# Adding an attention output bias on TensorE instead of GpSimd, with new instruction orders on all five engines

## The chip, the cores and the metric

One core of one Trainium2 chip runs the whole program. The metric is device time in microseconds (us) for one execution; three runs of the kernel before give the median. A span counted from the first to the last instruction is a little shorter than the device time. Engines are named as the profile names them: PE is TensorE's matmul side and PEld its weight loads, DVE is VectorE, ACT is ScalarE, POOL is GpSimd, SP is SyncE, which only issues transfers here. A trailing q (SPq) is an engine's queue.

## What is computed

Six blocks, each `x = layernorm(x + block(x))`, over x of 4 examples by 256 tokens by 256 features (8 tiles of 128 tokens):

```python
x = ln(x + attn0(x))     # linear attention, 16 heads: elu(q)+1, elu(k)+1; out @ o_w.T + o_b
x = ln(x + xattn0(x))    # 4 experts, chosen by token id: (silu(x Wg) * (x Wu)) Wd
x = ln(x + ffn0(x))      # 8 experts, all of them, weighted by "golden" weights
x = ln(x + attn1(x))     # 16 heads, causal softmax in groups of 32 tokens, half the heads rolled by 16
x = ln(x + xattn1(x))    # softmax over 256 memory rows of each example
x = ln(x + ffn1(x))      # 8 routed experts, top 2, and a shared one
```

Matrix products are done in three parts, with operands split into a high and a low part (hi·hi, hi·lo, lo·hi), to keep float32 accuracy. The change concerns `o_b`, the bias of the first attention's output product.

## The kernel before

The program is hand-written for the five engines, which meet only in semaphores. Tokens are handled in two halves of four tiles (h = 0, 1). The long part is a stream of 76 hidden chunks (chunk s = 0 to 75) in the three feed-forward blocks. For each chunk PE makes a gate product (step `g`) and an up product (step `u`, except in the first block, where the gate's input serves for both), six matmuls of 128x512 each; ACT takes silu (`s`); DVE multiplies (`m`, `hidden`); ACT writes the high part (`h`, `hidden_high`); POOL subtracts for the low part (`l`, `hidden_low`); PE multiplies by the down weights (`d`), and DVE adds the result to `x_tok` with an expert's weight (`a`). Weights come in raw by SP, are rounded to the high part by ACT and subtracted to the low part by POOL: steps `G` (gate and up weights of one pack), `D` (down weights) and `S` (weights of the second attention and of the memory rows); a number after the letter counts the packs, and on SP the same letter is the load itself. `X0` to `X3` do the same for the first block's experts.

Beside this stream run the steps with a dot, `letter half.number` (or `e example.number`): `b` the first attention, `n` and `r` layer norms and the golden routing, `e` norms and memory attention by example, `a h.i` the second attention and the last routing. `b h.9` is `a0_project`, the output product; `b1.8` transposes the attention output, which ACT and DVE split into `xp_hi` and `xp_lo`, for it. `p` are preparations at the start: DVE's `p5` converts the token ids into expert masks, and POOL's `p5` and `p6` are the two halves of the bias add. On DVE, `n h.0` (`a0_residual`, then `norm_stats`) adds the output product to `x_tok`; `r0.5` computes the golden weights, and `c` later constants.

What stands in what order on each engine is written out by hand in five lists: `SP_ORDER`, `PE_ORDER`, `ACT_ORDER`, `POOL_ORDER`, `DVE_ORDER`. Each engine walks its list; a step starts when the one ahead of it on the engine is done and its own semaphores are there, so a step that waits holds up all that stands behind it.

The output bias before: SP broadcasts `o_b` to all partitions (`bo1`, 128 KB). POOL adds it to the four tiles of each half of `x_tok` (L1241), and `a0_residual` waits for that (`x_biased`). The biases of keys and values already go another way: a weight operand `ones_r` with ones in three rows multiplies `b_kv`, whose row 0 holds the bias's high part and row 32 the low part, as one more matmul into the same accumulation (`ones_b`).

## Time and profile before

| | before |
|---|---|
| device time, median of three runs | 441.07 us |
| the three runs | 441.07, 441.37, 439.67 us |
| device time of the profiled execution | 441.07 us |
| its span, first to last instruction | 439.3 us |
| PE busy | 421.1 us |
| POOL, DVE, ACT busy | 271.5, 254.0, 246.9 us |

The profiled execution took 1.77 us more than its span, and its time is the median. Busy time says how full an engine was, not whether others waited for it; for PE the idle times in front of single instructions matter most, with what ended each. A matmul's modelled end lies behind the start of the next, so the idle time that a row shows is less than what the stream lost.

### The profile page before, as it was taken

To read this page: it belongs to the slowest core of one execution; us is meant where nothing else is said; L and a number is where in the kernel's file an instruction comes from. 1 tells how busy PE (TensorE), PEld (TensorE's weight loads), DVE (VectorE), ACT (ScalarE), POOL (GpSimd) and SP (SyncE) were. 2 spreads that over 40 slices of the span, in tenths; PEclk is the share of its full clock that TensorE was granted. 3 is DMA by queue.
4 is the path that set the end of the run, shared out by engine and by line. 5 is a ranking of instruction groups with operands and counts; after the bars stand their busy time and mean duration, and the time that the engine had idled before them with its cause. 6 is when DMAs were issued, how large, how long until landed. Compare 5 with 4: busy or idle time off the path is not lost.

```text
span 439.3 us, 9326 instructions
## 1 busy us (share of the span) xinstructions
PE 421.1 (96%) x3660; PEld 365.3 (83%) x3660; DVE 254.0 (58%) x641; ACT 246.9 (56%) x422; POOL 271.5 (62%) x237
## 2 busy tenths in 40 slices
...
DMA packets 15911, 35.32 MB, mean 80 GB/s; under 512 B 2139, under 2 KB 6235, under 8 KB 15868
## 3 DMA queue, kind: packets, MB, share of 16 engines
...
q8 instruction: 29, 0.48, 0.4%
q14 instruction: 14, 0.11, 0.1%
HBM read 33.15 MB, written 1.05 MB: 78 GB/s over the span
## 4 chain that ended last, share of the span: by engine, by line
PE 82%; DVE 10%; DMA 2%; issue 2%; ACT 2%; POOL 1%; SPq 1%; DVEq 0%; POOLq 0%; ACTq 0%
PE bank L455 13%; PE bank L456 13%; PE bank L458 13%; PE bank L717 8%; PE bank L719 7%; PE bank L718 7%; PE bank L736 2%; PE bank L793 1%; PE bank L781 1%; DVE hraw L1569 1%; DMA state<-o_tok 1%; PE bank L478 1%; DMA q_buf<-x_cols_dram 1%; PE bank L672 1%; PE bank L765 1%
## 5 line engine op out<-in xcount | busy, mean ns | idle before, releaser
L1257 POOL TENSOR_TENSOR h_lo<-hraw,h_hi 128x512 fp32r<-128x512 f32 x76 | 98.2, 1296 | 95.7 <-ACT h_hi L1048 95.7
L455 PE MATMUL bank<-xT_hi,pk_hi 128*128 128x512 f32 x256 | 103.3, 403 | 0.0
L456 PE MATMUL bank<-xT_hi,pk_lo 128*128 128x512 f32 x256 | 101.8, 398 | 0.8 <-issue 0.8
L1048 ACT ACTIVATE h_hi<-hraw 128x512 fp32r<-128x512 f32 x76 | 47.9, 630 | 76.6 <-DVE hraw L1569 72.6
L1263 POOL TENSOR_TENSOR pk_lo<-pk_raw,pk_hi 128x512 fp32r<-128x512 f32 (+1 forms) x44 | 74.6, 1696 | 10.3 <-ACT pk_hi L1066 10.3
L458 PE MATMUL bank<-xT_lo,pk_hi 128*128 128x512 f32 x256 | 80.9, 397 | 0.0
L717 PE MATMUL bank<-pk_hi,h_hi 128*128 128x256 f32 x272 | 77.9, 286 | 1.9 <-DVE x_tok L1583 1.3
L1569 DVE TENSOR_TENSOR hraw<-bank,sil 128x512 f32<-128x512 f32 x76 | 52.3, 689 | 45.9 <-ACT sil L1036 24.3
L719 PE MATMUL bank<-pk_hi,h_lo 128*128 128x256 f32 x272 | 76.8, 283 | 0.0
L718 PE MATMUL bank<-pk_lo,h_hi 128*128 128x256 f32 x272 | 76.8, 282 | 0.0
L458 PEld LDWEIGHTS bank<-xT_lo,pk_hi 128*128 128x128 f32 x256 | 48.5, 189 | 12.7 <-issue 1.0
L455 PEld LDWEIGHTS bank<-xT_hi,pk_hi 128*128 128x128 f32 x256 | 48.6, 190 | 10.3 <-issue 0.7
L1036 ACT ACTIVATE sil<-bank 128x512 f32<-128x512 f32 x76 | 44.7, 588 | 22.0 <-PE bank L458 21.9
L456 PEld LDWEIGHTS bank<-xT_hi,pk_lo 128*128 128x128 f32 x256 | 48.7, 190 | 10.1
L717 PEld LDWEIGHTS bank<-pk_hi,h_hi 128*128 128x128 f32 x272 | 51.8, 191 | 4.5 <-issue 2.3
L718 PEld LDWEIGHTS bank<-pk_lo,h_hi 128*128 128x128 f32 x272 | 51.9, 191 | 1.0
L719 PEld LDWEIGHTS bank<-pk_hi,h_lo 128*128 128x128 f32 x272 | 51.9, 191 | 0.0
L1268 POOL TENSOR_TENSOR pk_lo<-pk_raw,pk_hi 128x256 fp32r<-128x256 f32 (+1 forms) x44 | 41.5, 943 | 11.6 <-ACT pk_hi L1077 11.4
L1066 ACT ACTIVATE pk_hi<-pk_raw 128x640 fp32r<-128x640 f32 (+1 forms) x44 | 37.4, 849 | 18.2 <-PE bank L458 14.5
L1077 ACT ACTIVATE pk_hi<-pk_raw 128x256 fp32r<-128x256 f32 (+1 forms) x44 | 21.6, 492 | 28.1 <-PE bank L719 27.9
L1583 DVE SCALAR_TENSOR_TENSOR x_tok<-bank,gold,x_tok 128x256 f32<-128x256 f32 x64 | 27.4, 477 | 13.5 <-PE bank L719 13.5
L1549 DVE TENSOR_TENSOR sil<-bank,sil 128x512 f32<-128x512 f32 x22 | 15.2, 690 | 34.5 <-ACT sil L1036 17.7
...
## 6 DMA issues: line engine op xcount, KB each, us to landing
...
```

The lines of the kernel that those rows point to most:

```text
L455: pe.matmul(o, w(kc)[0], x(kc)[0], start=kc == 0, stop=False)
L456: pe.matmul(o, w(kc)[1], x(kc)[0], start=False, stop=False)
L458: m = pe.matmul(o, w(kc)[0], x(kc)[1], start=False, stop=kc == KC - 1)
L717: pe.matmul(o, hh, vh, start=closed and kc == 0, stop=False, skip_group_check=not closed)
L718: pe.matmul(o, hh, vl, start=False, stop=False, skip_group_check=not closed)
L719: m_ = pe.matmul(o, hl, vh, start=False, stop=closed and kc == chunks - 1, skip_group_check=not closed)
L1036: A(sil[:, s % 2, :], src[:, :], ACT.Silu).then_inc(sems["silu_done"], 1)
L1048: A(h_hi[:, row, at * 512:(at + 1) * 512], hraw[:, s % 2, :], ACT.Copy).then_inc(sems["hid_hi"], 1)
L1257: pool.tensor_tensor(h_lo[:, row, q], hraw[:, s % 2, :], h_hi[:, row, q].bitcast(F32), ALU.subtract).then_inc(sems["hid_lo"], 1)
L1263: pool.tensor_tensor(g_part(kind, i, pk_lo)[:, 0:w], raw_g(kind, i)[0][:, 0:w], g_part(kind, i, pk_hi)[:, 0:w].bitcast(F32), ALU.subtract) ...
L1268: pool.tensor_tensor(d_part(kind, i, pk_lo), raw_d(kind, i)[0], d_part(kind, i, pk_hi).bitcast(F32), ALU.subtract).then_inc(sems["d_lo"], 1)
L1569: TT(hraw[:, r, :], other[:, :], sil[:, r, :], ALU.mult).then_inc(sems["hid_mul"], 1)
```

## The change

The bias moves into the output product. `b_o`, a 128x256 slice of a buffer that is free then, gets the high part of `o_b` in row 0 (an additional ACT copy in `p0`) and the low part in row 32 (an additional DVE subtraction in `p0`), and `a0_project` gets one more matmul of 128x256 for each of the eight tiles. The row of biases grows from 512 to 768 columns. SP's broadcast of `o_b`, POOL's two adds and their semaphores go; `a0_residual` waits for `x_tok` itself to be loaded.

All five lists are written anew, most of their lines differing. The diff, with two lines of each kind of the lists:

```diff
 SP_ORDER = """
-G0 D0 G1 D1 S0 G2 D2 G3 D3 G4 D4 G5 S1 D5 ...
+S0 G0 D0 G1 D1 S1 G2 D2 G3 D3 G4 D4 G5 D5 ...
...
 POOL_ORDER = """
-p1 p5 p3 p4 p6 X0 X1 X2 X3 n0.0 G0 D0 l0 l1 n1.0 ...
+p1 p3 p4 n0.0 X0 X1 X2 X3 l0 l1 n1.0 l2 l3 l4 l5 S0 l6 l7 l8 G0 D0 ...
...
-        bo1 = sb("bo1", [P, D])
-        brow = sb("brow", [P, 2 * D])
+        brow = sb("brow", [P, 3 * D])
+        b_o = pr_lo[:, 0, :]
...
-            sp.dma_start(bo1[:, :], bias_o.partition_broadcast(P)).then_inc(sems["in_bo"], 16)
...
-                        m = pe.matmul(o, al, wh, start=False, stop=kc == KC - 1)
+                        pe.matmul(o, al, wh, start=False, stop=False)
+                    m = pe.matmul(o, ones_r, b_o, start=False, stop=True)
...
-                    A(b_kv[0:BZ, :], brow[0:BZ, :], ACT.Copy).then_inc(sems["bz_hi"], 1)
+                    A(b_kv[0:BZ, :], brow[0:BZ, 0:2 * D], ACT.Copy).then_inc(sems["bz_hi"], 1)
+                    A(b_o[0:BZ, :], brow[0:BZ, 2 * D:3 * D], ACT.Copy).then_inc(sems["bz_hi"], 1)
...
-                if i >= 5:
-                    q = slice(HT * (i - 5), HT * (i - 4))
-                    pool.wait_ge(sems["in_x"], 16)
-                    pool.wait_ge(sems["in_bo"], 16)
-                    pool.tensor_tensor(x_tok[:, q, :], x_tok[:, q, :], bo1[:, :].unsqueeze(1).to_broadcast([P, HT, D]),
-                                       ALU.add).then_inc(sems["x_biased"], 1)
...
-                    dve.wait_ge(sems["bz_hi"], 1)
-                    TT(b_kv[GS:BZ, :], brow[GS:BZ, :], b_kv[GS:BZ, :].bitcast(F32), ALU.subtract
+                    dve.wait_ge(sems["bz_hi"], 2)
+                    TT(b_kv[GS:BZ, :], brow[GS:BZ, 0:2 * D], b_kv[GS:BZ, :].bitcast(F32), ALU.subtract)
+                    TT(b_o[GS:BZ, :], brow[GS:BZ, 2 * D:3 * D], b_o[GS:BZ, :].bitcast(F32), ALU.subtract
                        ).then_inc(sems["bz_lo"], 1)
...
-                dve.wait_ge(sems["x_biased"], h + 1)
+                if h == 0:
+                    dve.wait_ge(sems["in_x"], 16)
```

Three places of the lists matter below. First DVE, where the first attention ends and the first block begins. Before, `n0.2` (`xT_lo`), then `p5` (the eight small instructions), then `b1.8` (`xp_lo`) and `m0`, `m1` (`hraw`):

```order
L1411 TENSOR_TENSOR xT_lo<-bank,xT_hi 128x2x256 x2
L1444 RECIPROCAL temp<-temp 128x1
L1445 CAST ids_f<-ids_i 128x8
L1448 TENSOR_SCALAR route<-ids_f 128x8
L1450 TENSOR_SCALAR s<-ids_f 128x8
L1451 SCALAR_TENSOR_TENSOR route<-ids_f,s 128x8
L1450 TENSOR_SCALAR s<-ids_f 128x8
L1451 SCALAR_TENSOR_TENSOR route<-ids_f,s 128x8
L1452 TENSOR_SCALAR route<-ids_f 128x8
L1539 TENSOR_TENSOR xp_lo<-bank,xp_hi 128x512 x2
L1569 TENSOR_TENSOR hraw<-bank,sil 128x512 x2
```

and now:

```order
L1407 TENSOR_TENSOR xT_lo<-bank,xT_hi 128x2x256 x2
L1537 TENSOR_TENSOR xp_lo<-bank,xp_hi 128x512 x2
L1440 RECIPROCAL temp<-temp 128x1
L1441 CAST ids_f<-ids_i 128x8
L1444 TENSOR_SCALAR route<-ids_f 128x8
L1446 TENSOR_SCALAR s<-ids_f 128x8
L1447 SCALAR_TENSOR_TENSOR route<-ids_f,s 128x8
L1446 TENSOR_SCALAR s<-ids_f 128x8
L1447 SCALAR_TENSOR_TENSOR route<-ids_f,s 128x8
L1448 TENSOR_SCALAR route<-ids_f 128x8
L1567 TENSOR_TENSOR hraw<-bank,sil 128x512 x2
```

`p5` moved behind `xp_lo`, and still stands ahead of `hraw`.

Second ACT at the same place of the program. Before, from the second half's attention queries on (`b1.3`, `G0`, `n0.1`, `n0.2`, `D0`, `b1.8`, `s0`, `h0`, `s1`, `h1`):

```order
L1023 ACTIVATE q_buf<-bank,bcol 128x512
L1066 ACTIVATE pk_hi<-pk_raw 128x1024 [waits raw_g0]
L961 ACTIVATE x_tok<-x_tok,shift,rstd 128x256 [waits ln_rstd]
L961 ACTIVATE x_tok<-x_tok,shift,rstd 128x256 x3
L937 ACTIVATE xT_hi<-bank 128x2x256 [waits xt_ps] x2
L1077 ACTIVATE pk_hi<-pk_raw 128x512 [waits raw_d0]
L1027 ACTIVATE xp_hi<-bank 128x512 [waits a0_aT_ps] x2
L1036 ACT_TABLE_LOAD
L1036 ACTIVATE sil<-bank 128x512 [waits gate_ready]
L1048 ACTIVATE h_hi<-hraw 128x512 [waits hid_mul]
L1036 ACTIVATE sil<-bank 128x512 [waits gate_ready]
L1048 ACTIVATE h_hi<-hraw 128x512 [waits hid_mul]
```

and now:

```order
L938 ACTIVATE xT_hi<-bank 128x2x256 [waits xt_ps] x2
L1029 ACTIVATE xp_hi<-bank 128x512 [waits a0_aT_ps] x2
L1038 ACT_TABLE_LOAD
L1038 ACTIVATE sil<-bank 128x512 [waits gate_ready]
L1068 ACTIVATE pk_hi<-pk_raw 128x1024 [waits raw_g0]
L1079 ACTIVATE pk_hi<-pk_raw 128x512 [waits raw_d0]
L1050 ACTIVATE h_hi<-hraw 128x512 [waits hid_mul]
L1038 ACTIVATE sil<-bank 128x512 [waits gate_ready]
L1050 ACTIVATE h_hi<-hraw 128x512 [waits hid_mul]
L1085 ACTIVATE wa_hi<-kv_buf 128x2x768 [waits a0_o_ps,raw_s]
L1038 ACTIVATE sil<-bank 128x512 [waits hid_mul,gate_ready]
```

`G0` and `D0` moved in between the first silu and the first `h_hi`, and `S0` (`wa_hi<-kv_buf`), which stood behind `s8`, behind the second `h_hi`.

Third PE in the second attention's first half. Before, the end of the queries' product (`a0.3`) and the start of the keys' (`a0.4`):

```order
L458 MATMUL bank<-xT_lo,wa_hi 128x512 x2
L455 MATMUL bank<-xT_hi,wa_hi 128x512 [waits a1_q]
L456 MATMUL bank<-xT_hi,wa_lo 128x512
L455 MATMUL bank<-xT_hi,wa_hi 128x512
L456 MATMUL bank<-xT_hi,wa_lo 128x512
```

and now:

```order
L458 MATMUL bank<-xT_lo,wa_hi 128x512 x2
L455 MATMUL bank<-xT_hi,pk_hi 128x512 [waits silu_done,g_lo]
L456 MATMUL bank<-xT_hi,pk_lo 128x512
L455 MATMUL bank<-xT_hi,pk_hi 128x512
L456 MATMUL bank<-xT_hi,pk_lo 128x512
L458 MATMUL bank<-xT_lo,pk_hi 128x512 x2
L455 MATMUL bank<-xT_hi,wa_hi 128x512 [waits a1_q]
```

The gate product `g35` moved from ahead of `a0.3` to between the two. In the same way `g36` moved to between `a0.6` and `a0.7`, and `e0.12`, `e1.12` from behind `g34` to ahead of it; in the second half of the tokens `a1.3` and `a1.4`, and `a1.6` and `a1.7`, still follow each other directly.

## Rows read from the trace of the kernel before

**Rows 1.** The page: busy share of the engines, and the chain that ended last.
```profile
PE 421.1 (96%) x3660; PEld 365.3 (83%) x3660; DVE 254.0 (58%) x641; ACT 246.9 (56%) x422; POOL 271.5 (62%) x237
PE 82%; DVE 10%; DMA 2%; issue 2%; ACT 2%; POOL 1%; SPq 1%; DVEq 0%; POOLq 0%; ACTq 0%
```
**Rows 2.** The timeline, output product `b0.9`: start, duration, engine, line, instruction.
```profile
28.88 0.28 PE L592 MATMUL bank<-wa_hi,h_hi 128*128 128x256 f32 x1
28.99 0.28 PE L593 MATMUL bank<-wa_lo,h_hi 128*128 128x256 f32 x1
```
**Rows 3.** The timeline, from `n0.2` to `b1.9`; idle time in brackets.
```profile
41.01 1.28 DVE L1411 TENSOR_TENSOR xT_lo<-bank,xT_hi 128x512 fp32r<-128x512 f32 x2
...
42.20 0.15 DVE L1444 RECIPROCAL temp<-temp 128x1 f32<-128x1 f32 x1
...
44.25 1.29 DVE L1539 TENSOR_TENSOR xp_lo<-bank,xp_hi 128x512 fp32r<-128x512 f32 x2
...
45.59 0.39 PE L592 MATMUL bank<-wa_hi,xp_hi 128*128 128x256 f32 x1 [1.21 <-DVE xp_lo L1539]
```
**Rows 4.** The timeline: `X2`, `X3` low parts, `n0.0`, `G0`, `l0`, `S0`.
```profile
28.83 2.54 POOL L1232 TENSOR_TENSOR xp_lo<-pk_raw,xp_hi 128x512 fp32r<-128x512 f32 x2
...
34.85 1.02 POOL L1217 TENSOR_TENSOR rstd<-var_e,mhalf 128x4 f32<-128x4 f32 x1 [3.49 <-DVE var_e L1380]
...
35.91 1.06 ACT L1066 ACTIVATE pk_hi<-pk_raw 128x1024 fp32r<-128x1024 f32 x1
...
46.88 1.29 POOL L1257 TENSOR_TENSOR h_lo<-hraw,h_hi 128x512 fp32r<-128x512 f32 x1 [3.80 <-ACT h_hi L1048]
...
66.39 1.48 ACT L1083 ACTIVATE wa_hi<-kv_buf 128x1536 fp32r<-128x1536 f32 x1
```
**Rows 5.** The view of L375, SP's loads of gate packs: issue to landing.
```profile
DMA to landing us min/median/max: 3.5/3.7/5.5
```
**Rows 6.** The timeline: a bias add on POOL, and DVE beside the other.
```profile
16.04 1.00 DVE L1524 SCALAR_TENSOR_TENSOR q_buf<-kx,q_buf 128x512 f32<-128x512 f32 x1 [1.56 <-ACT q_buf L1023]
...
21.54 2.40 POOL L1241 TENSOR_TENSOR x_tok<-x_tok,bo 128x1024 f32<-128x1024 f32 x1
```
**Rows 7.** The timeline: the norm `r1.0` on DVE, then `d9` on PE.
```profile
110.02 1.34 DVE L1380 TENSOR_SCALAR var_e<-mv 128x4 f32<-128x4 f32 x1
110.04 1.30 POOL L1268 TENSOR_TENSOR pk_lo<-pk_raw,pk_hi 128x512 fp32r<-128x512 f32 x1
...
112.28 0.36 PE L717 MATMUL bank<-pk_hi,h_hi 128*128 128x256 f32 x1 [0.50 <-DVE x_tok L1583]
```
**Rows 8.** The timeline: `D7` and `l31` on POOL, `d14` and `d15` on PE.
```profile
161.09 0.35 PE L717 MATMUL bank<-pk_hi,h_hi 128*128 128x256 f32 x1 [0.76 <-DVE x_tok L1583]
...
162.16 1.30 POOL L1268 TENSOR_TENSOR pk_lo<-pk_raw,pk_hi 128x512 fp32r<-128x512 f32 x1
163.42 1.28 POOL L1257 TENSOR_TENSOR h_lo<-hraw,h_hi 128x512 fp32r<-128x512 f32 x1
...
164.80 0.35 PE L717 MATMUL bank<-pk_hi,h_hi 128*128 128x256 f32 x1 [0.61 <-issue]
```
**Rows 9.** The timeline, PE: start of `a0.3`, of `a0.4` and of `a0.7`.
```profile
178.85 0.47 PE L455 MATMUL bank<-xT_hi,wa_hi 128*128 128x512 f32 x1 [0.19 <-issue]
...
182.72 0.50 PE L455 MATMUL bank<-xT_hi,wa_hi 128*128 128x512 f32 x1 [0.84 <-DVE q_buf L1647]
...
196.29 1.56 PE L781 MATMUL bank<-kx,q_buf 64*32 64x128 f32 x64 [0.58 <-DVE kv_buf L1664]
```
**Rows 10.** The timeline at `a0.11`; busy time of PE, PEld, DVE, ACT, POOL, clock, DMA.
```profile
224.00 0.58 SPq L375 DMA_DIRECT2D pk_raw<-pk_f_dram  x1
...
226.98 0.27 PE L793 MATMUL bank<-kv_buf,pT 32*32 32x17 f32 x10 [1.05 <-issue]
...
227.00:231.00 4.00, 4.00 (x20) 3.15 (x20) 1.97 (x4) 1.49 (x3) 1.28 (x1) 0.57 0.04 13
```
**Rows 11.** The timeline, PE: start of `e3.2`.
```profile
340.88 0.84 PE L478 MATMUL bank<-con,x_tok 128*128 128x128 f32 x4 [0.39 <-ACT x_tok L951]
```

More of the change, by code:

```diff
@@ L113 @@
 SP_ORDER = """
[L114 to L115 removed]
+S0 G0 D0 G1 D1 S1 G2 D2 G3 D3 G4 D4 G5 D5 G6 D6 G7 D7 G8 D8 G9 D9 G10 D10 G11 S2 D11 G12 S3 D12 G13 D13 G14 D14 R0 G15
+R1 D15 G16 G17 G18 S4 G19 G20 G21 G22 G23 G24 G25 G26 R2 G27 R3 G28 G29 G30 G31 G32 G33 G34 G35 G36 G37 G38 G39 G40
 G41 G42 G43 O0
```

86 lines of the change are left out of this document (42 added, 44 removed).

## Prediction, made before the changed kernel ran

> **What bounds the kernel now.** I read the busy line and the chain first [rows 1]: PE is busy for 421.1 of 439.3 us, and 82% of the chain that ended last is PE, 10% DVE. So the time is PE's own work, plus the places where PE waits, plus a start and an end that the change leaves alone. An engine at 56 to 62% counts only where PE waits for it. A matmul that is added to PE costs its whole length; one that is moved costs nothing by itself. After that I read, instruction by instruction, the rows of PE that show idle time, and for each what stands ahead of the releaser on its own engine.
>
> How much an idle row is worth: in the output product the starts of 128x256 matmuls lie 0.12 us apart (28.88 to 28.99, and on average 0.12), while one is modelled with 0.28 us [rows 2]. Idle time counts from that modelled end, so a wait has cost the stream 0.16 us more than its row shows. I use this for all rows of PE below.
>
> **The added matmuls.** Eight of 128x256 at 0.12 us: +0.96 us. Nothing hides them. The four in `b0.9` also push everything behind it, since queries, state and norm follow from it in a chain; the four in `b1.9` come after.
>
> **The small pieces in p0.** An additional ACT copy and an additional DVE subtraction on 33 rows and 1 row. No row has them. Between nothing and one 128x512 DVE instruction (0.64, half of the pair in [rows 3]) they delay the key and value biases; I take 0, since a row-wide instruction of half that width is about 0.4 and the first matmul that needs them comes later than that after the existing subtraction. Upper bound: +0.3.
>
> **What goes from POOL.** Two adds of 2.40 us each [rows 6]. PE waits for neither, and nothing of weight is queued behind them. Beside the first one DVE's `q_buf` instruction took 1.00 us [rows 6], and the second of its kind there waits for ACT anyway. Value: 0; it could be up to 0.3 if some instruction beside them was on the chain. The broadcast load is worth nothing either.
>
> The Trainium skill ("SBUF — State Buffer", section "Who interferes with whom") says that GpSimd and VectorE share one port pair, held exclusively for a whole instruction. By that rule the long `q_buf` instruction is one that waited for the bias add, and its gain is real but off the path, as the sum has it.
>
> **p5 behind b1.8 on DVE.** Before, the id conversion ran from 42.20 to 44.25, between `xT_lo` and `xp_lo`, and PE stood idle for 1.21 us in front of `b1.9` [rows 3], so it lost 1.37. Now `xp_lo` follows `xT_lo`: it ends at 42.29 + 1.29 = 43.6, plus 0.48 of bias matmuls 44.1. PE is due at 45.59 - 1.37 + 0.48 = 44.7. The wait is gone: **-1.37**. Next late is PE itself. The 2 us of `p5` now lie ahead of the first `hraw`; that one then ends near 46.8, before PE's `g2`, which needs it at about 48.1.
>
> **G0 and D0 ahead of h0 on ACT.** Here the new order has a price. POOL made the low parts of `X2`, `X3` before 31.4 [rows 4], and SP issued the loads of `G0` and `D0` then. Now `n0.0` stands ahead of all four: it begins at 34.85 + 0.48 and takes 1.3 us with its second instruction, then four times 1.27 us (half of 2.54) end at 41.7. The load of `G0` is issued then and lands 3.7 us later, 3.5 at best and 5.5 at worst [rows 5]: at 45.4. ACT then rounds `G0` (1.06) and `D0` (about 0.6) and only then takes `h0`, at 47.2 or a little later, instead of 46.2. `h0`, `s1`, the product on DVE and `h1` follow in turn (four steps of about 0.65), then `l1` with 1.29 [rows 4]: done near 51.3. PE is due at `d0` at 44.7 + 28 times 0.12 + 2.8 for `g2`, `g3` = 50.9. That is a wait of 0.35 (0.1 of it already at `g3`). Behind `h1` now stands `S0`, 1.48 us [rows 4], and the second norm's `n1.1` comes later by that and by the later `h` steps: `n1.2` on PE loses about 0.6. Together **+0.95**.
>
> **The norm r1.0 and d9.** Before, `a8` stood behind `r1.0` and PE lost 0.50 + 0.16 at `d9` [rows 7]. Now `a8` stands ahead of it, and PE reaches `d9` later; but `m20` stands behind the norm and `u22` needs it. The norm's small DVE instructions are slow only while POOL works: `var_e` took 1.34, from 110.02 until POOL's instruction of 110.04 ended at 111.34 [rows 7]. With POOL busy for one of the two such instructions I get a wait of 0.3 at `u22`, with both 1.3, with none 0. **-0.66 + 0.3**.
>
> **D7, l31, d14, d15.** `r1.5` and `a13` stay as they were, and so does the wait in front of `d14` [rows 8]. At `d15` POOL did `D7` (1.30) ahead of `l31`, which could have started about 0.4 earlier; `D7` now is done before it. **-0.4**.
>
> **The second attention.** The start of `a0.3` at 178.85 hangs on DVE's constants and low parts, not on PE; now `g35` (six matmuls, 1.4) is still owed at that point, and the transposes of `e1.12` moved ahead wait as well. Between `a0.3` and `a0.4` PE lost 0.84 + 0.16 = 1.0 [rows 9], which `g35` now fills: +1.4 - 1.0 = **+0.4**. Between `a0.6` and `a0.7` it lost 0.58 + 0.16 [rows 9], and `g36` covers all of it: **-0.74**. The second half's pair of such waits has nothing put in and stays. At `e3.2` PE lost 0.39 + 0.16 [rows 11]; two down products now stand between the earlier steps and it: **-0.55**.
>
> **The sum.** +0.96 - 1.37 + 0.95 - 0.36 - 0.4 + 0.4 - 0.74 - 0.55 = **-1.11 us**. The profiled run took 441.07, of which 439.3 is span, and is itself the median: 441.07 - 1.11 = 440.0. With the open prices at their ends (0.3 of `p0`, -0.3 on POOL, `u22` 0 to 1.3, the load 3.5 to 5.5) the forecast's own range is 438.7 to 441.6.
>
> **Rivals.** (A) *The instruction stall does not come back.* In `a0.11` PE stood for 1.05 us ("issue") while a load issued at 224.00 was in flight, and in the four us from 227 on the granted clock was 0.57, between the two levels of 1.2 and 2.4 GHz [rows 10]. That cost 1.2 + 4 x 0.43 = 2.9 us. PE's order there is unchanged and `D13`, `G14`, `G15` keep their places, which speaks for a repetition; but a shift of 1 us between load and matmuls may dissolve it, and one of the three runs was 1.4 us below the median. Time: 437.1.
>
> (B) *The gain at b1.9 does not come.* `b1.9` could wait for ACT's `xp_hi` or for the first norm instead. The rows show ACT ahead of DVE there, which speaks against. Then only the matmuls and the loads' order are left: 440.0 + 1.37 = 441.4.
>
> (C) *ACT's queue stands behind weights that are not there, the slower side.* If `G0` lands after 5.5 us instead of 3.7, `h0`, `l1` and `d0` come 1.8 later, all of it on PE; `D0`, issued behind it, can land up to 0.4 later still, and the same pattern comes again where `D2`, `G3` stand ahead of `h18`, for about 0.8 at `g21`. 440.0 + 3.0 = 443.0. It decides from a landing after about 46 us. The load is alone with that of `S0`, which speaks against.
>
> Where a page's rule would give another time: the skill's rule of the exclusive port would make both small instructions of `r1.0` wait if POOL has `l18` and `l19` back to back. That is the upper end (1.3 at `u22`), inside the forecast; the trace agrees with it at 110.02.
>
> **Chances.** Forecast 0.45, A 0.25, B 0.15, C 0.15. 0.5% (2.2 us) is about what a measurement of this kernel can tell from no change: 438.9 and 443.3 are the bounds. Faster: A and a little of the forecast, 0.30. Slower: the upper half of C and what I overlook in 2000 moved rows, 0.12. Same: 0.58. The range for 8 in 10 takes in A at its centre and most of C: 437.0 to 442.9; the forecast's own range stands above.
>
> **What would show each step.** Eight matmuls with `pr_lo` in the output products, 0.12 apart. No idle time in front of the second product's first matmul. `G0`'s rounding on ACT starting near 45.5, `h0` at 47.2, a short wait of PE before the first `L718` matmul, and one at the transposes of `n1.2`. No idle before `d9`, a short one at `u22`. `a0.3` waiting and `a0.4` not; `a0.7` not; in the second half both still idle with 0.84 and 0.58. The stall in `a0.11` and the clock after it as before. The forecast is wrong if a new idle time of over 1 us stands anywhere in PE's row, above all between 46 and 60 us, or if the stall and the low clock are gone.

## The result, and the profile after

| | before | after |
|---|---|---|
| median | 441.22 us (4 runs, 439.67 to 441.51) | 448.05 us (4 runs, 446.67 to 448.8) |
| profiled execution | 441.07 | 447.0 |
| its span | 439.3 | 445.2 |

The ratio is 1.0152, with a 95% interval of 1.0122 to 1.0182: the change costs 6.8 us. Forecast were 440.0, and 437.0 to 442.9. The record lists 23 executions of the changed kernel in all; without the two slow ones (452.24 and 452.65) their median is 447.51, so the four of the table lie about 0.5 high, and with them what is counted from 448.05 below. The page of the profile after begins with these busy times; the last line is from the chain that ended last [rows 1]:

```profile
PE 425.5 (96%) x3668; PEld 368.0 (83%) x3668; DVE 256.1 (58%) x642; ACT 247.3 (56%) x423; POOL 265.5 (60%) x235
...
PE 70%; DVE 10%; ACT 6%; POOL 5%; DMA 4%; issue 3%; SPq 1%; ACTq 0%; DVEq 0%; POOLq 0%
```

POOL lost its two adds and is 6.0 us less busy. PE's share of the chain fell from 82% to 70%: other engines now stand in it. To find where, I compared PE's start times at the points at which both kernels have done the same set of steps. The time is the start of the next step, with its wait. How much later the changed kernel is there:

| both have done everything up to | before, us | later by |
|---|---|---|
| `b0.1` | 13.1 | +1.14 |
| `b0.9` | 31.7 | +1.59 |
| `g1`, ahead of `b1.9` | 45.6 | +0.20 |
| `g5` | 58.0 | +1.89 |
| `u20` | 112.3 | +1.22 |
| `u31`, then `d14` | 161.1, 164.8 | +2.27, +2.87 |
| `e1.12`, then `u34` | 175.6, 177.1 | +3.66, +5.07 |
| `a0.3` | 182.7 | +3.72 |
| `a0.6` | 196.3 | +2.88 |
| `a0.26` | 232.9 | +2.12 |
| `d25`, then `a1.10` | 307.2, 317.5 | +2.39, +3.12 |
| `g60`, then `e3.7` | 358.5, 360.9 | +4.16, +4.87 |
| `a1.24`, and at the end | 376.1 | +5.89, +5.95 |

No single place did it. Some gains came as forecast, and about ten losses of 0.3 to 1.6 us came too, most of them not in the sum. The timeline's rows (start, duration, engine, line, instruction; idle time in brackets) show each kind once.

**At the start** the new one-row subtraction in `p0`, and the bias matmul of `b0.1` behind it:

```profile
9.42 1.29 POOL L1229 TENSOR_TENSOR wa_lo<-pk_raw,wa_hi 128x512 fp32r<-128x512 f32 x1 [7.95 <-ACT wa_hi L972]
9.46 1.53 DVE L1473 TENSOR_TENSOR pr_lo<-brow,pr_lo 1x256 fp32r<-1x256 f32 x1
...
11.13 0.47 PE L494 MATMUL bank<-pr_hi,pr_lo 128*128 128x512 f32 x1 [0.41 <-DVE pr_lo L1473]
```

256 numbers took VectorE 1.53 us. POOL's instruction had started 0.04 earlier, and the small one ended 0.28 after it.

**At the first block** ACT waits for the load of `G0`, then for that of `D0`, and only then takes `h0` (L1050) [rows 4, 5]; PE waits at `g3` and `d0`:

```profile
46.93 1.06 ACT L1068 ACTIVATE pk_hi<-pk_raw 128x1024 fp32r<-128x1024 f32 x1 [0.84 <-DMA pk_raw<-pk_f_dram]
...
48.55 0.63 ACT L1079 ACTIVATE pk_hi<-pk_raw 128x512 fp32r<-128x512 f32 x1 [0.56 <-DMA pk_raw<-pk_f_dram]
...
49.09 0.61 ACT L1050 ACTIVATE h_hi<-hraw 128x512 fp32r<-128x512 f32 x1
...
50.97 0.50 PE L455 MATMUL bank<-xT_hi,pk_hi 128*128 128x512 f32 x1 [0.26 <-DVE hraw L1567]
...
53.00 0.39 PE L718 MATMUL bank<-pk_hi,h_hi 128*128 128x256 f32 x1 [0.38 <-POOL h_lo L1253]
```

**In the routing** `r1.5` on VectorE two tiny instructions took 1.32 and 1.19 us instead of 0.19 and 0.17, each beside a POOL instruction (`D7`, `l29`). Before, only one of `r1.5` was long, `none_in` with 1.26 us. Now `d14` starts behind 1.82 us of idle time instead of 0.76 [rows 8]. Below it the windows from 161 us on, in the columns of [rows 10] (PE, PEld, DVE, ACT, POOL, granted clock, DMA share, GB/s):

```profile
156.74 1.29 POOL L1264 TENSOR_TENSOR pk_lo<-pk_raw,pk_hi 128x512 fp32r<-128x512 f32 x1 [2.98 <-ACT pk_hi L1079]
156.75 1.32 DVE L1610 TENSOR_TENSOR fb<-fb,pick 128x32 f32<-128x32 f32 x1
...
158.21 1.29 POOL L1253 TENSOR_TENSOR h_lo<-hraw,h_hi 128x512 fp32r<-128x512 f32 x1 [0.18 <-ACT h_hi L1050]
158.33 1.19 DVE L1612 TENSOR_SCALAR s<-s 128x4 f32<-128x4 f32 x1
...
163.36 0.36 PE L718 MATMUL bank<-pk_hi,h_hi 128*128 128x256 f32 x1 [1.82 <-DVE x_tok L1581]
```

```profile
161.00:163.00 2.00, 0.54 (x3) 0.10 (x1) 1.86 (x7) 0.54 (x2) 0.00 (x0) 1.00 0.01 4
163.00:165.00 2.00, 1.64 (x12) 1.67 (x13) 1.59 (x4) 0.95 (x3) 1.29 (x1) 0.89 0.00 0
165.00:167.00 2.00, 2.00 (x11) 2.00 (x11) 0.87 (x2) 0.25 (x1) 1.67 (x2) 0.50 0.00 0
```

Behind PE's pause the granted clock fell to 0.50, the lower of its two levels (1.2 instead of 2.4 GHz). This fall belongs to that execution: nine profiles of the experiments below have the same order here and the same 1.99 to 2.00 us lost at `d14`, and a granted clock of 1.00 behind it. In them `d15` still loses 0.41 to 0.43 and `e1.12` 1.24 to 1.26; in the profile of the changed kernel the stretch at the low clock hid all of the first and part of the second (0.51).

**At the second attention** `S1`'s low part on POOL lies on VectorE's constants `c`: the instruction L1455 took 1.64 us, before 0.69. `a0.3` (L455) stands behind 1.34 us of idle time [rows 9]:

```profile
176.39 2.37 POOL L1274 TENSOR_TENSOR xp_lo<-kv_buf,xp_hi 128x1024 fp32r<-128x1024 f32 x1
...
177.67 1.64 DVE L1455 TENSOR_SCALAR cap<-cap 128x1024 f32<-128x1024 f32 x1
...
182.18 0.47 PE L455 MATMUL bank<-xT_hi,wa_hi 128*128 128x512 f32 x1 [1.34 <-issue]
```

**Late in the second half** order alone costs. On POOL, `e3.1`'s two tiny instructions (L1219, L1220) stand behind the low parts of `D25` and `G26` though VectorE had their input (L1389) at 340.05, and PE waits at `e3.2` [rows 11]. On ACT the silu `s62` stands behind `G33`, which waits 3.76 us until PE's `u62` frees its room; the product `g64` waits for it:

```profile
339.89 0.16 DVE L1389 TENSOR_SCALAR var_e<-mv 128x2 f32<-128x2 f32 x1
339.91 1.28 POOL L1259 TENSOR_TENSOR pk_lo<-pk_raw,pk_hi 128x512 fp32r<-128x512 f32 x1
341.15 0.71 POOL L1219 TENSOR_TENSOR rstd<-var_e,mhalf 128x2 f32<-128x2 f32 x1
...
342.91 0.84 PE L478 MATMUL bank<-con,x_tok 128*128 128x128 f32 x4 [0.79 <-ACT x_tok L952]
...
377.97 0.74 ACT L1068 ACTIVATE pk_hi<-pk_raw 128x640 fp32r<-128x640 f32 x1 [3.76 <-PE bank L458]
...
380.33 0.60 ACT L1038 ACTIVATE sil<-bank 128x512 f32<-128x512 f32 x1
...
381.96 0.48 PE L455 MATMUL bank<-xT_hi,pk_hi 128*128 128x512 f32 x1 [0.86 <-DVE hraw L1567]
```

### The profile page after: what moved, and what is told of

It reads as the page before. It is cut to its first block, busy times and chain, and to the rows that moved or that the text cites. A ratio compares the mean times of both kernels' runs of the same rounds, so it can differ in the third digit from the quotient of the medians.

```text
span 445.2 us, 9339 instructions
## 1 busy us (share of the span) xinstructions
PE 425.5 (96%) x3668; PEld 368.0 (83%) x3668; DVE 256.1 (58%) x642; ACT 247.3 (56%) x423; POOL 265.5 (60%) x235
## 3 DMA queue, kind: packets, MB, share of 16 engines
HBM read 33.05 MB, written 1.05 MB: 77 GB/s over the span
## 4 chain that ended last, share of the span: by engine, by line
PE 70%; DVE 10%; ACT 6%; POOL 5%; DMA 4%; issue 3%; SPq 1%; ACTq 0%; DVEq 0%; POOLq 0%
PE bank L455 12%; PE bank L456 11%; PE bank L458 11%; PE bank L718 7%; PE bank L720 7%; PE bank L719 7%; DMA pk_raw<-w_attn_dram 1%; PE bank L782 1%; DVE stats L1383 1%; DVE hraw L1567 1%; DMA state<-o_tok 1%; PE bank L737 1%; PE bank L794 1%; DMA pk_raw<-pk_f_dram 1%; ACT L1038 1%
## 5 line engine op out<-in xcount | busy, mean ns | idle before, releaser
L455 PE MATMUL bank<-xT_hi,pk_hi 128*128 128x512 f32 x256 | 103.0, 402 | 1.4 <-DVE hraw L1567 1.1
L1050 ACT ACTIVATE h_hi<-hraw 128x512 fp32r<-128x512 f32 x76 | 47.8, 629 | 77.4 <-DVE hraw L1567 72.1
L718 PE MATMUL bank<-pk_hi,h_hi 128*128 128x256 f32 x272 | 78.8, 290 | 2.2 <-DVE x_tok L1581 1.8
L455 PEld LDWEIGHTS bank<-xT_hi,pk_hi 128*128 128x128 f32 x256 | 48.5, 189 | 12.8 <-issue 1.7
L719 PEld LDWEIGHTS bank<-pk_lo,h_hi 128*128 128x128 f32 x272 | 52.8, 194 | 0.9
```

Of the source, the lines that this page charges most:

```text
L455: pe.matmul(o, w(kc)[0], x(kc)[0], start=kc == 0, stop=False)
L718: pe.matmul(o, hh, vh, start=closed and kc == 0, stop=False, skip_group_check=not closed)
L719: pe.matmul(o, hh, vl, start=False, stop=False, skip_group_check=not closed)
L1050: A(h_hi[:, row, at * 512:(at + 1) * 512], hraw[:, s % 2, :], ACT.Copy).then_inc(sems["hid_hi"], 1)
```

## Experiments

Ratios are to the kernel before, run on the same chip in the same rounds, with 95% intervals. The changed kernel itself didn't run in these rounds, so a gain against it is a difference of two such ratios. Single executions of one kernel spread over 2 to 7 us, so of effects under 1.5 us the traces tell more than the medians. "Lost" is what PE's start-to-start spacing exceeds its usual one by.

### The two halves of the change, and its late half

`e1`: all five new lists, bias by POOL.

```diff
-p1 p3 p4 n0.0 X0 X1 X2 X3 ...
+p1 p5 p3 p4 p6 n0.0 X0 X1 X2 X3 ...
```

> All five new orders, with the bias still added by GpSimd (its two adds stand where they stood before, ahead of the first low parts) and no bias matmuls. Theory 1 (most of the loss comes from what the new orders put beside and ahead of each other): about 4.8 us over the kernel before, 446.0, since of the 6.8 us lost the bias part explains 0.96 for the matmuls and about 1.1 for its two small pieces at the start. Theory 2 (the bias part delays the start, and the orders lose only because they then meet the engines in other phases): within 1 us of the kernel before. In the trace theory 1 wants the waits before d14, a0.3 and g64 to be there, theory 2 wants them gone.

448.4 us, ratio 1.0154 [1.0113, 1.0196]: the orders alone cost what the whole change costs, and more than the 4.8 us of theory 1. The waits before `d14`, `a0.3` and `g64` are there.

`e2`: the bias as matmuls, lists of before (POOL without `p5`, `p6`).

> The bias as matmuls, with the orders of before (less the two GpSimd adds). Theory 1: the matmuls cost 8 x 0.12 = 0.96, and the small subtraction of the low part of o_b (one row of 256), which took 1.53 us beside a GpSimd instruction in the changed kernel, costs 0.57 more, and the first two products another 0.5: +2.0 over the kernel before, 443.2. The prediction's own view (the small pieces are free): +0.96, 442.2. Rival: the bias part is the whole loss, 447 or more.

441.55 us, ratio 1.0006 [0.9978, 1.0033]. PE is 1.10 us later than before at the end of `b0.1`, and 2.05 after `b1.9`; at `u20`, where before it waited, 0.66 is absorbed, and 0.91 is left at the end. So the bias part is a small cost, and not the loss. The +2.0 us of theory 1 lie outside the interval (-1.0 to +1.5), the +0.96 inside it.

`e4`: the changed kernel, from about 240 us with the lists of before.

```diff
 PE    ... u46 g47 
-u47 d22 e0.7 e1.7 d23 a0.22 g48 u48 g49 u49 e2.12 e3.12 g50 u50 ...
+e0.7 u47 d22 e1.7 d23 a0.22 g48 u48 g49 u49 g50 u50 e2.12 e3.12 ...
```

> The changed kernel up to about 240 us, and from there on the five lists of before (from u47 on PE, G16 on ACT and POOL, a22's neighbour e0.7 on VectorE). Theory 1 (each place loses by its own local order): the 3.8 us that PE's stream lost between 232 us and the end go, -3.8 against the changed kernel, 444.2. Theory 2 (the late waits are the echo of the 2 us by which PE was already late there, or of weights that come later): at most 1 us is won, 447 or more.

441.81 us, ratio 1.0002 [0.9979, 1.0026]. Theory 1 wins: the late half costs 4.0 us between the two traces, as it asked, and 6.2 in the medians (5.7 against 447.51). By the medians the first 240 us of the change net nothing, within about 1 us; by its trace `e4` is 1.9 us behind the kernel before there, and 2.0 at the end.

### The late half in pieces

`e9`: one step of ACT.

```diff
-h61 G31 a1.22 D31 G32 D32 G33 D33 s62 a1.24 h62
+h61 G31 a1.22 D31 G32 s62 D32 G33 D33 a1.24 h62
```

> The changed kernel with one step moved on ScalarE: s62 back ahead of D32. Theory (G33 on ScalarE waits for weight room that PE's u62 gives back, and s62, whose gate product is done at 376.5, stands behind it until 380.3): s62 near 376.5, no wait in front of g64, -1.0, 447.0. Rival: g64 waits for the low parts of G33 next, which GpSimd makes at 378.8 to 380.1, or m62 waits for VectorE's a1.23: under 0.3 is won.

446.03 us, ratio 1.0133 [1.0064, 1.0201]; the median alone doesn't decide it. The trace speaks against the rival: in it `s62` starts at 376.07, as soon as its product is there, the wait at `g64` is gone, and PE gains 1.1 us at that place and keeps it:

```profile
376.07 0.60 ACT L1038 ACTIVATE sil<-bank 128x512 f32<-128x512 f32 x1 [1.32 <-PE bank L458]
```

`e10`: the lists of before for the memory attention's stretch alone.

```diff
 ACT   ... G23 D23 h53 s54 G24
-D24 G25 h54 s55 h55 s56 e2.1 h56 s57 D25 G26 e2.2 e3.1 e3.2 D26 G27 D27 G28 D28 h57 ...
+h54 s55 D24 G25 D25 G26 h55 s56 h56 D26 G27 e2.1 e3.1 e2.2 e3.2 s57 h57 s58 ...
```

> The changed kernel with the lists of before for the stretch of the second half's memory attention alone (PE from a1.11 to u60, ScalarE and GpSimd from D24 on, VectorE from m55 to o60). Theory (the losses at e3.2, e3.5 and e3.7 are of this stretch's own order, the weight steps D26 to D28 put ahead of h57 among them): 2.2 us, the sum of what the trace lost there, 445.8; the wait at g64 stays. Rival: the losses come in from ahead of the stretch (a1.10, g54), and under 0.7 is won.

445.02 us, ratio 1.0097 [1.0055, 1.0139]. The losses at `e3.2` (0.95), `e3.5` (0.53) and `e3.7` (0.32) are gone, and PE gains 2.5 us between `d29` and `u60`. The wait at `g64` stays.

`e16`: the lists of before from 232 to 326 us alone.

> The changed kernel with the lists of before for the stretch from 232 to 326 us alone (PE from e0.7 to a1.25/u54, ScalarE from G16 or S3 on, GpSimd from G16, VectorE from e0.7; SP's S4 behind G22). Theory (besides the 0.5 lost at g54 and 0.5 at the memory transposes, the changed order puts a1.10's burst of small matmuls ahead of d28 and stalls there by 2.6 us in some executions, as in two of eight profiles of such orders, which the medians see and the profile of the changed kernel does not): 1 us in the trace and 2 to 3 in the median, 445 to 446. Rival (the three parts of the late lists only win together): under 1, 447.5.

446.18 us, ratio 1.0095 [1.0066, 1.0125]: 2.5 us by the ratios. Its trace gains 1.1 up to `d28`; then instruction stalls of 0.90 and 1.19 at `a1.25` and `a1.11` took it back in that execution. The theory's stall at `a1.10` is not the order's: it stands in two of nine profiles with the new order there (2.58 in `e1`, 2.84 in `e6`), and in one of ten with the old (1.98 in `e3`). Against 447.51 the median gains 1.3 us, about what the trace shows; against 448.05 some 0.5 more, for which no trace speaks. The three pieces give 0.19, 0.55 and 0.57% by the ratios, together 1.31%; `e4` gave 1.50%. With intervals of 0.3 to 0.7% each, this neither shows nor excludes that they simply add up.

### The early places

`e17`: everything about the first weights as before. `e8` had been a first try, which moved `G0`, `D0` and `S0` on ACT and `n0.0` on POOL, but not `X0` to `X3` on ACT, nor the load of `S0`, which the change put ahead of that of `G0`.

```diff
 SP, e17 only
-S0 G0 D0 G1 D1 S1
+G0 D0 G1 D1 S0 S1
 ACT, e17 only
-b1.0 b0.8 b1.1 p4 X0 X1 X2 X3
+p4 b1.0 X0 X1 b0.8 X2 X3 b1.1
 POOL (e17: also G0 D0 ahead of l0, S0 behind l8)
-n0.0 X0 X1 X2 X3
+X0 X1 X2 X3 n0.0
 ACT, both
-n0.1 n0.2 b1.8 s0 G0 D0 h0 s1 h1 S0 ...
+G0 n0.1 n0.2 D0 b1.8 s0 h0 s1 h1 ... s8 S0
```

> The changed kernel with the first weights where they stood: G0 ahead of n0.1 and D0 ahead of b1.8 on ScalarE, S0 behind s8 there, and n0.0 behind X3 on GpSimd. Theory (G0 and D0 ahead of h0 made h0 49.1 instead of 46.2, and cost 0.42 at g3 and 0.54 at d0): both waits go, PE is 1.0 us earlier at 55 us, 447.0 if all of it is kept. Rival: n0.0 behind X3, or S0 behind s8, makes another wait (the first norm, n1.2) and the gain is under 0.3; or the later wait at d14 takes it back.

457.81 us, ratio 1.0364 [1.0325, 1.0403], 10 us worse. SP issued `G0` only at 39.06, behind `S0`, which waits for the attention's state, and ACT stood in front of `G0` with the norm behind it:

```profile
38.69 0.33 SPq L387 DMA_DIRECT2D kv_buf<-w_attn_dram  x1
39.06 0.43 SPq L375 DMA_DIRECT2D pk_raw<-pk_f_dram  x1
...
44.47 1.06 ACT L1068 ACTIVATE pk_hi<-pk_raw 128x1024 fp32r<-128x1024 f32 x1 [7.06 <-DMA pk_raw<-pk_f_dram]
```

That cost PE 5.55 us, in front of `n0.2`. The other large loss, 3.97 at `g10`, has a second cause: on POOL `S0` had been left ahead of `l6` while ACT's `S0` went behind `s8`, so POOL stood still and `l6` with it:

```profile
75.88 3.45 POOL L1270 TENSOR_TENSOR wa_lo<-kv_buf,wa_hi 128x1536 fp32r<-128x1536 f32 x1 [6.06 <-ACT wa_hi L1085]
```

> The changed kernel with everything about the first weights as before: on ScalarE the stretch from p4 to s8 (X0 to X3 early, G0 ahead of n0.1, D0 ahead of b1.8, S0 behind s8), on GpSimd n0.0 behind X3, G0 and D0 ahead of l0, S0 behind l8, and on SP the load of S0 behind D1. In e8 SP issued G0's load only at 39.06, behind that of S0 at 38.69, which waits for the attention state, and ScalarE stood 7.06 us in front of G0. Theory: the loads are issued near 31.5 again, no wait at n0.2, g3, d0 and g10, -1.0 in the trace at 55 us, 447.1. Rival: S0's low part on GpSimd, or the second load S1 on SP, is now late and G2's load with it: a wait at g10 or later of over 1 us.

445.23 us, ratio 1.0080 [1.0055, 1.0104]. So the theory holds and the rival, a wait of over 1 us at `g10` or later, didn't come. The load is issued at 32.56, and the waits at `g3` and `d0` are gone: 1.3 us in the trace between `b1.8` and `g5`. The ratio gained 0.72%, 3.2 us (2.3 against 447.51). Against `e9`, which is the changed kernel up to 370 us, 0.9 more show up at 225 us, but that is a smaller stall in `a0.25` (1.09 lost instead of 1.97), and not the order; what the medians have beyond the 1.3 stays unexplained.

`e7`: `D7` and `G8` back behind `h29`.

```diff
 ACT
-h28 s29 D7 G8 h29 s30 h30 s31 h31 D8
+h28 s29 h29 s30 h30 s31 D7 h31 G8 D8
 POOL
-D7 l29 l30 l31
+l29 l30 D7 l31
```

> The changed kernel with D7 and G8 on ScalarE back where they stood (D7 behind s31, G8 behind h31) and D7 on GpSimd back behind l30. Theory (GpSimd's D7 and l29, now free to run at 156.7 to 159.5, fall on two tiny instructions of the routing r1.5 on VectorE, which make r1.5 a microsecond longer and d14 late): r1.5 takes 6.9 us again, d14 loses about 0.8 instead of 1.98, the granted clock of 0.5 behind it is gone: -1.1 to -1.7 where it stands, 446.5 if the rest of the way keeps it. Rival 1 (l29 falls into r1.5 wherever D7 is, since it comes when h29 comes): r1.5 stays at 7.9 us and nothing is won, 448. Rival 2: d14 is won, and the later wait at a0.3, which hangs on VectorE, takes it back: 448 with a0.3 losing 2.5 instead of 1.5.

445.73 us, ratio 1.0114 [1.0051, 1.0177], which alone can't be told from the changed kernel. In the trace `r1.5` is a microsecond shorter: of its small instructions only one meets POOL, as before the change, and `d14` loses 0.94 instead of 1.98. At `d15` 0.76 comes back, as before the change. About 0.7 is left at `e0.12`, and rival 2 didn't come (`a0.3` loses 1.52 as before). The low clock, the second hope of the expectation, was no loss of the order: it was the profiled execution's own, about 1 us.

```profile
154.84 1.29 POOL L1253 TENSOR_TENSOR h_lo<-hraw,h_hi 128x512 fp32r<-128x512 f32 x1 [0.88 <-ACT h_hi L1050]
...
154.89 1.27 DVE L1608 TENSOR_SCALAR none_in<-s 128x4 f32<-128x4 f32 x1
...
162.51 0.35 PE L718 MATMUL bank<-pk_hi,h_hi 128*128 128x256 f32 x1 [0.77 <-DVE x_tok L1581]
```

`e6`: `S1` back behind `s34` on ACT and `l33` on POOL. `e11`: also `S2` behind `s35` and `l34`.

```diff
 ACT (e11)
-s18 S1 D2 ... h33 s34 S2 a0.4 D10 G11 h34 s35 h35
+s18 D2 ... h33 s34 S1 a0.4 D10 G11 h34 s35 S2 h35
```

> The changed kernel with S1, the first weights for the memory attention, back behind s34 on ScalarE and behind l33 on GpSimd. Theory (S1's low part on GpSimd at 176.4 to 178.8 lies on VectorE's constants c and makes them 5.8 us long instead of 4.7): c takes 4.7 us, a0.3 loses 0.4 instead of 1.51, -1.1, 446.9. Rival: the wait at a0.3 is for the low parts of the normed input, which come after c on VectorE and hang on GpSimd's other work too; then c shrinks by under 0.4 and the time stays, 448.

452.36 us, ratio 1.0251 [1.0192, 1.0310]. The theory was right on VectorE (`cap` 0.69 us, `bk_four` 0.23, and `a0.3` loses nothing) and wrong on the sum: `S2`'s load is issued when `S1`'s low part is done, and on ACT `S2` stood ahead of `a0.4`, on which `a0.5` waits:

```profile
176.87 0.69 DVE L1454 TENSOR_SCALAR cap<-cap 128x1024 f32<-128x1024 f32 x1
177.60 0.23 DVE L1455 TENSOR_SCALAR bk_four<-con,bcol 128x4 f32<-128x4 f32 x1
...
192.55 1.06 ACT L1091 ACTIVATE xp_hi<-kv_buf 128x1024 fp32r<-128x1024 f32 x1 [6.25 <-DMA kv_buf<-pk_x_dram]
...
196.43 0.55 PE L765 MATMUL bank<-wa_hi,xT_hi 128*128 128x256 f32 x1 [5.15 <-ACT kx L1115]
```

> The changed kernel with both memory weights moved: S1 behind s34 (ScalarE) and l33 (GpSimd) as in e6_S1_back, and S2 behind s35 and l34, so that ScalarE's a0.4 no longer stands behind S2. Theory (e6's 5.31 us in front of a0.5 came from S2, which stood ahead of a0.4 on ScalarE and waited 6.25 us for a load that is issued only when S1's low part is done; the constants c are 4.7 us or less without S1 beside them, as e6 showed with 3.7): no wait at a0.5, a0.3 without its 1.51, 1.3 us won at 200 us, 446.8. Rival (a0.5 waits for the moved keys for another reason, say the transfers between partitions): the wait at a0.5 stays above 2.

447.32 us, ratio 1.0137 [1.0091, 1.0183]. Neither `a0.3` nor `a0.5` waits, and 1.5 us are won up to `a0.7`; then `d17` loses 1.10, since `l35` now comes behind `S2`'s low part on POOL and ends at 200.5. The rival didn't come. Each of these steps had been placed for the others.

### The small subtraction, and PE's stalls

`e5`: `e2`, with `o_b`'s low subtraction as a step of its own behind `b0.7` on VectorE.

```diff
-                    dve.wait_ge(sems["bz_hi"], 2)
-                    TT(b_kv[GS:BZ, :], ..., ALU.subtract)
-                    TT(b_o[GS:BZ, :], ..., ALU.subtract).then_inc(sems["bz_lo"], 1)
+                    dve.wait_ge(sems["bz_hi"], 1)
+                    TT(b_kv[GS:BZ, :], ..., ALU.subtract).then_inc(sems["bz_lo"], 1)
+                elif i == 6:
+                    dve.wait_ge(sems["bz_hi"], 2)
+                    TT(b_o[GS:BZ, :], ..., ALU.subtract).then_inc(sems["bz_lo"], 1)
```

> The bias as matmuls with the orders of before, as in e2_matmul_alone, and in addition the small subtraction of o_b's low part taken out of the start: it is a step of its own on VectorE behind b0.7, with its own count, and only the output product waits for it. Theory (in e2 this one-row subtraction took 1.52 us, since it starts beside a GpSimd subtraction of 1.28, and PE's stream stood 1.10 us behind the kernel before at the end of b0.1): the one-row subtraction takes about 0.4 in its new place, PE is within 0.2 of the kernel before at the end of b0.1, so 0.9 earlier than in e2; of this some 0.7 may be lost again at later waits, as e2 lost 2.0 by 49 us and had 0.9 of it at the end: 440.8 to 441.5, e2 less 0 to 0.9. Rival (the additional ScalarE copy, which pushes the next weights' high part by 0.4, is what is late): under 0.3 is won at b0.1.

440.20 us, ratio 0.9976 [0.9949, 1.0003]: the theory holds at `b0.1`, the rival doesn't, and the median is a little below the range that was expected. The same instruction in the two kernels, `e2` first:

```profile
9.43 1.52 DVE L1472 TENSOR_TENSOR pr_lo<-brow,pr_lo 1x256 fp32r<-1x256 f32 x1
```

```profile
23.99 0.41 DVE L1476 TENSOR_TENSOR pr_lo<-brow,pr_lo 1x256 fp32r<-1x256 f32 x1
```

At the end of `b0.1` PE is 1.17 us ahead of `e2` and level with the kernel before.

`e13`: the kernel before, with six loads cut to 64 columns; it leaves the rest of these weights out and serves for the stalls alone.

```diff
-                    sp.dma_start(to, pk_f0[i % E0, :, 0:G_F0]).then_inc(landed, 16)
+                    n = 64 if i >= 13 else G_F0
+                    sp.dma_start(to[:, 0:n], pk_f0[i % E0, :, 0:n]).then_inc(landed, 16)
```

> The kernel before, in which the loads of the last three packs of the first routed block (G13 to G15, D13 to D15) carry 64 columns each instead of 1024 and 512; the packs keep old weights in the rest, so this kernel leaves that part of the weights out and its time is read only for PE's stalls. Theory (transfers of weights beside PE's many small matmuls delay its instructions): the two stalls of 1.00 and 1.23 us lost at u40 and in a0.11 go, and the low clock behind them, 3 us less, 438. Rival (the burst of small matmuls runs PE out of instructions by itself, since another run of the changed orders stalled 2.4 us at a1.10 with a DMA share of 0.00 to 0.04): the stalls stay, within 0.3 us each, 441.

441.73 us, ratio 1.0015 [0.9983, 1.0048]: the rival holds. The stalls stand where they stood, with 1.07 and 1.21 us lost, and so does the idle time of 1.04 in `a0.11` (1.05 in [rows 10]). The windows from 225 us on, of the kernel before and then of `e13`:

```profile
225.00:227.00 2.00, 0.94 (x114) 0.84 (x103) 0.00 (x0) 0.00 (x0) 0.83 (x1) 1.00 0.83 244
227.00:229.00 2.00, 2.00 (x15) 1.64 (x15) 1.28 (x3) 0.35 (x1) 0.00 (x0) 0.65 0.08 27
```

```profile
225.00:227.00 2.00, 0.96 (x106) 0.85 (x94) 0.00 (x0) 0.00 (x0) 0.70 (x1) 1.00 0.08 17
227.00:229.00 2.00, 2.00 (x18) 1.63 (x11) 1.28 (x3) 0.47 (x1) 0.00 (x0) 1.00 0.03 8
```

With a DMA share of 0.08 instead of 0.83 the pause is the same, so the weight loads beside it don't make it. That the burst runs PE out of instructions by itself, as the rival says, no view shows. The same pause was followed by a clock of 0.65 once, and of 1.00 once.

### Towards a kernel that beats both

`e3`: the kernel before, `p5` behind `b1.8` on VectorE.

> The kernel before with one step moved: VectorE's id conversion p5 stands behind the low part of the attention output (b1.8) and no longer ahead of it. Theory: the wait of PE before b1.9 (row: 1.21 us idle, 1.37 lost) goes and nothing is late in its place, -1.4 us, 439.8. Rival: the first feed-forward chunk's hraw, now behind p5, or the norm waits instead and takes it back: 0, 441.2.

440.01 us, ratio 0.9948 [0.9917, 0.9978]. The wait at `b1.9` is gone and nothing took its place: 1.37 in the trace.

`e12`: the same, and PE's other waits filled.

```diff
-a0.3 a0.4 u35 d16 a0.5 a0.6 a0.7 d17 g36 ... a1.3 a1.4 g51 u51 a1.5 a1.6 a1.7 g52 ... e2.2 e3.2 d32
+a0.3 u35 a0.4 d16 a0.5 a0.6 g36 a0.7 d17 ... a1.3 g51 a1.4 u51 a1.5 a1.6 g52 a1.7 ... e2.2 d32 e3.2
```

> The kernel before, with work put into its waits: p5 behind b1.8 on VectorE as in e3_p5_alone, and on PE the up product u35 between a0.3 and a0.4, g36 ahead of a0.7, g51 between a1.3 and a1.4, g52 ahead of a1.7 and the down product d32 ahead of e3.2. No bias matmul. Theory (each wait is filled by a product whose inputs are there already): -1.4 for p5, -1.0 (a0.4), -0.74 (a0.7), -1.0 (a1.4), -0.74 (a1.7), -0.55 (e3.2): -5.4, 435.6 against 441.0. Rival 1 (attention's chain on VectorE and ScalarE ends last, and a later product of it waits by as much as the filled one came later): only p5's gain, 439.2. Rival 2 (a step that was pushed back, as m35 and d16 behind u35, becomes late): a little above rival 1.

448.87 us, ratio 1.0169 [1.0130, 1.0209]. Only `u35` helped for good. `g36` waited 3.23 us for its pack's low part, `g51` lost 2.02 and behind them `a1.5` and `a1.8` lost 1.54 and 1.75. A product fills a wait only if its own inputs are there.

```profile
196.64 0.80 PE L455 MATMUL bank<-xT_hi,pk_hi 128*128 128x512 f32 x1 [3.23 <-POOL pk_lo L1263]
```

`e14` is `e3` with `u35` between `a0.3` and `a0.4`; `e15` is `e5` with `p5` behind `b1.8`; `e18` is `e15` with `u35` moved as well.

> The kernel before with p5 behind b1.8 (as e3_p5_alone) and the up product u35 between a0.3 and a0.4 on PE. Theory (u35's inputs are there, in e12 it won 1.1 us and what lost there were g36, g51 and g52, which waited for silu, low parts and products not yet made): -1.4 and -1.0 in the trace, the wait at a0.4 gone, 438.9 or lower against 441.2. Rival: m35 and s35, now later, make g36 or d17 wait for as much: as e3, 439.9.

439.30 us, ratio 0.9949 [0.9922, 0.9977]: the wait is gone in the trace (1.0 us), 0.32 is lost at `a0.5` instead, and 0.8 is gained up to `u40`, but the ratio is that of `e3`; an effect of this size is too small for these intervals.

> The kernel before with p5 behind b1.8, the bias as matmuls, and o_b's low subtraction behind b0.7 (e3 and e5 together). Theory (both are local, and the matmuls cost 0.96 at the start, some of it absorbed at the later wait of e3.2, while GpSimd is 4.8 us freer): -1.4 + 0.5 to 0.9 in the trace, 440.0 to 440.6. Rival (the freed GpSimd is worth something, as e5's 0.24% below the kernel before hints): below e3, 439.5 or less.

438.88 us, ratio 0.9934 [0.9906, 0.9962]. The median is where the rival wants it, but the intervals of `e3` and `e15` overlap, and the traces don't show that a freer GpSimd is worth something: up to `a1.10` `e15` is 1.6 us behind `e3`, which then loses 1.98 in a stall. That stays open.

> The kernel before with the bias as matmuls, o_b's low subtraction behind b0.7, p5 behind b1.8 (all as in e15) and u35 between a0.3 and a0.4 (as in e14). Theory: the wait at a0.4 (1.00 lost) goes in this kernel too, e15 less 0.7 to 1.0: ratio 0.991 to 0.992 to the kernel before, about 438.0. Rival (e14's median was no better than e3's, the gain is given back at a0.11 and after): as e15, 0.9934.

438.50 us, ratio 0.9923 [0.9898, 0.9948]. This beats both kernels, the one before by 0.77% or 3.4 us. From 0.9934, which the rival named, it can't be told apart.

## Why the prediction was wrong

Beside each term of the forecast stands what the traces of the two kernels show at its place, by the starts of PE's steps:

| place | forecast, us | traced, us |
|---|---|---|
| start, up to `b0.1` | 0 | +1.14 |
| eight bias matmuls | +0.96 | +0.86 |
| `b1.9`, by `p5` | -1.37 | -1.38 |
| `g2` to `g5`, by `G0` and `D0` | +0.95 | +1.30 |
| `d9` and `u22` | -0.36 | -0.65 |
| `d14` | 0 | +1.05 |
| `d15`, with the low clock there | -0.40 | +0.60 |
| `e0.12` to `a0.3` | +0.40 | +0.85 |
| `a0.7` | -0.74 | -0.73 |
| stalls, up to `a0.26` | 0 | -0.76 |
| from there to the end | -0.55 | +3.83 |
| small differences | | -0.16 |
| sum | -1.11 | +5.95 |

**Right, with its size.** The matmuls with `pr_lo` lie 0.12 apart and cost 0.48 and 0.38 in the two halves. `p5` behind `b1.8`: -1.39 (forecast -1.37), confirmed alone by `e3`. `a0.7`: -0.74. No idle time at `d9`: -0.65 (forecast -0.66); the wait of 0.3 that the forecast put at `u22` didn't come. No wait at `a0.4`, and both waits of the second half unchanged.

**"The small pieces in p0 ... I take 0 ... Upper bound: +0.3"** was outside its own bound: 0.57 is lost at the bias matmul of `b0.1`, and `e2` lost 1.17 there against `e5`. Over all profiles, PE ends `b0.1` at 13.98 to 14.63 in the eleven kernels with this subtraction in `p0`, and at 12.93 to 13.33 in the nine without it, bias matmuls or not. The step took the duration of such an instruction alone (0.4), which is right (0.41 in `e5`), and did not ask what POOL has at that moment. The prediction had the mechanism in hand for `r1.0` and did not use it here. The Trainium skill ("SBUF — State Buffer", section "Who interferes with whom") says that an instruction of VectorE with two inputs in SBUF contends with one of GpSimd that reads SBUF, and that the order of issue, not the shape, decides who waits; this trace agrees, one row of 256 waiting with 1.53 us.

**"G0 and D0 ahead of h0", +0.95**, was right in its cause: 1.3 by `g5`, and 1.3 back in the trace of `e17`. That the size is near is in part luck. Of the 0.95, 0.35 were for the wait at `g3` and `d0`, which lost 0.96 (0.42 and 0.54), and 0.6 for `n1.2`, where nothing was lost. `G0` landed at 46.9, not 45.4, and `h0` came at 49.1, not 47.2: the load took its 3.6 us, but was issued at 43.33 instead of 41.7, since the start was late and `n0.0` took 1.9 us on POOL instead of 1.3.

**"r1.5 and a13 stay as they were, and so does the wait in front of d14"** failed, +1.05. The steps on VectorE were unchanged, but the prediction itself says that `D7` moved on POOL, and it did not ask beside which instructions of VectorE `D7` and `l29` would now run. `e7` put it back and the microsecond went. That `d15` gains was right: 0.34 in the nine other profiles with this order (forecast 0.4); the 0.77 of the changed kernel's own profile come from the low clock, which let the wait vanish and cost more than it.

**`a0.3`, +0.4** came as +0.8 (from +2.9 behind `d15` to +3.72 behind `a0.3`): 0.51 is lost at `e1.12` and 1.51 at `a0.3`, and the 1.00 of `a0.4` is saved. In the seven other profiles that have this order and leave `S1` alone it is about +1.5, since `e1.12` loses 1.25 in them. The step said that the start "hangs on DVE's constants and low parts", and then took their end from the old trace. `S1`'s new place made them 1.1 us longer; `e6` made them shorter again.

**`e3.2`, -0.55** came as +0.4: the step counted the down products in front of PE's wait and not the two weight steps that the same lists put in front of `e3.1` on POOL.

**What the sum did not have** is most of the result, and the step that failed most: behind `a0.26` it had one term, the -0.55 of `e3.2`, and everything else that the new lists do there stood at nothing. PE fell back by 3.8 us in the trace, mostly at `g54` (0.50), `e3.2` (0.95), `e3.5` (0.53), `e3.7` (0.54) and `g64` (1.02); by `e4` it is 4.0 in the traces and 5.7 to 6.2 in the medians. The prediction gave "what I overlook in 2000 moved rows" a part of 0.12. The trace of before has hardly a wait of PE there, and from that I read that nothing is to be gained or lost; but a place without waits is one that the old order had fitted.

**The forecast's own range**, 438.7 to 441.6, doesn't follow from the ends that it names: these give 439.2 (nothing at `u22`, -0.3 for POOL, a landing after 3.5 us) to 443.1 (+0.3, 1.3 at `u22`, a landing after 5.5 us). The result lies outside both.

**Rival A**: the stall of `a0.11` did not come, another came at `a0.25` (1.62 lost) with a clock of 0.50 behind it, and the net from `a0.7` to `a0.26` was -0.8. By `e13` the weight loads don't make it. **Rival B** did not come. **Rival C** was to be decided by a landing after 46 us, and `G0` did land at 46.9, but by a late issue and not by a slow load, and neither the 1.8 us of it nor the 0.8 at `g21` came. It named the right kind of cause, a step that stands behind weights that are not there, at the wrong place; `e8` and `e6` show it at its full price, 5.5 and 5.3 us lost at one wait, and `s62` behind `G33` at 1.1.
